# The causal layer's block solve: one PSUM bank for all heads, and hops as four full-array matmuls

## What is computed

```
logits = jnp.einsum('bhqd,bhkd->bhqk', q, k) * scale
probs = jax.nn.softmax(logits + causal_mask, axis=-1)
L = jnp.eye(s) - jnp.tril(probs, -1)
rhs = jnp.diagonal(probs, axis1=-2, axis2=-1)[..., None] * v
A = solve_triangular(L, rhs, lower=True)
out = A.transpose(0, 2, 1, 3).reshape(b, s, HID) @ Wd.T + bd
```

## Time and profile before

| what | value |
|---|---|
| median of 3 runs | 1507.68 us |
| the runs | 1501.56, 1507.68, 1512.19 us |
| span of the profiled execution | 1507.1 us |
| PE busy | 1237.4 us (82%) |
| DVE busy | 1035.0 us (69%) |
| ACT busy | 729.2 us (48%) |
| POOL busy | 628.0 us (42%) |
| mean granted clock of TensorE | 0.883 |

### The profile page before, as it was taken

The page is one execution under the profiler, slowest core; times in us unless marked ns, Lnnn a source line. Parts: engine busy times, 40 slices in busy tenths (PEclk is TensorE's granted clock), DMA queues, the critical chain, the costliest instruction groups (busy, mean ns, idle before and its releaser), DMA issues. The chain is left out here.

```text
span 1507.1 us, 30851 instructions
## 1 busy us (share of the span) xinstructions
PE 1237.4 (82%) x11642; PEld 673.8 (45%) x11642; DVE 1035.0 (69%) x2290; ACT 729.2 (48%) x1596; POOL 628.0 (42%) x838
## 2 busy tenths in 40 slices
PE   6656677779999988538889988988988799999976
PEld 2212232222333337424666766666666333333276
DVE  6699999979888955457446646645632588988653
ACT  3834334317766675313524523533442166676754
POOL 2279888853424215314423423223332524351244
PEclk9878888869999998758889879978997599999988
DMA  5378833023224022441421231141120231331213
GB/s 166 145 274 320 298 139 140 20 67 87 55 65 122 13 82 63 100 86 23 88 38 25 45 74 28 21 100 18 18 51 10 67 79 31 97 89 45 81 48 88
DMA packets 137737, 128.41 MB, mean 85 GB/s; under 512 B 92007, under 2 KB 123559, under 8 KB 132202
## 3 DMA queue, kind: packets, MB, share of 16 engines
q1 hardware_dynamic: 129536, 118.56, 28.6%
q0 software_dynamic: 2496, 5.13, 1.1%
q10 hardware_dynamic: 5558, 2.76, 0.9%
HBM read 105.61 MB, written 38.62 MB: 96 GB/s over the span
## 5 line engine op out<-in xcount | busy, mean ns | idle before, releaser
L1393 DVE TENSOR_REDUCE f_row_min<-f_ps 128x1 f32<-128x512 f32 x512 | 323.9, 676 | 55.6 <-PE f_ps L1720 55.2
L1283 ACT ACTIVATE f_e<-f_ps 128x512 f32<-128x512 f32 x512 | 282.8, 602 | 126.4 <-PE f_ps L1740 122.5
L1720 PE MATMUL f_ps<-f_operands 72*128 72x512 bf16 x512 | 205.4, 410 | 26.4 <-DMA f_operands<-k_scr 15.4
L1740 PE MATMUL f_ps<-f_operands 75*128 75x512 bf16 x512 | 189.5, 380 | 2.6 <-ACT f_e L1283 2.1
L790 PE MATMUL m_ps<-m_shared,sb_ident 128*128 128x512 f32 x256 | 136.8, 683 | 58.1 <-DVE m_shared L630 58.0
L363 POOL TENSOR_TENSOR m_drive<-m_du,m_ring 128x1024 f32<-128x1024 f32 x64 | 149.7, 2352 | 56.2 <-DVE m_ps L622 37.6
L495 ACT ACTIVATE m_ps<-m_delta,m_A 128x511 f32<-128x511 f32 x128 | 83.0, 681 | 131.7 <-DVE m_ps L622 109.0
L1751 PE MATMUL f_ps<-f_e,f_v_op 128*32 128x512 f32 x1024 | 136.4, 604 | 2.1 <-ACT f_e L1283 1.4
L2714 DVE TENSOR_TENSOR d_aT<-d_ps,d_aT 128x16 f32<-128x16 f32 x224 | 37.9, 169 | 140.9 <-PE d_ps L2892 140.7
L1720 PEld LDWEIGHTS f_ps<-f_operands 72*128 72x128 bf16 x512 | 51.3, 101 | 181.2 <-DVE f_row_min L1393 127.3
L2545 DVE TENSOR_REDUCE d_row_min<-d_ps 128x1 f32<-128x384 f32 (+3 forms) x176 | 106.3, 634 | 35.9 <-PE d_ps L2786 34.7
(11 more groups left out here) (298 smaller groups left out, 2345.3 us busy)
## 6 DMA issues: line engine op xcount, KB each, us to landing
m_ring<-bc_scr SPq DMA_DIRECT2D x32, 1024.0 KB, 5.4
f_rows_scr<-blank SPq DMA_DIRECT2D x2, 8707.5 KB, 30.8
f_wall<-f_wall SPq DMA_DIRECT2D x16, 578.0 KB
f_operands<-q_scr SPq DMA_DIRECT2D x32, 288.0 KB
f_operands<-k_scr SPq DMA_DIRECT2D x96, 96.0 KB
d_q_op<-q_scr SPq DMA_DIRECT2D x6, 576.0 KB
d_k_op<-k_scr SPq DMA_DIRECT2D x18, 192.0 KB
f_operands<-f_rows_scr SPq DMA_DIRECT2D x46, 64.5 KB, 1.8
```

What stands on the lines that cost most here:

```text
L1283: nc.scalar.activation(e_sb[:, n % 3, hh, :], ps[:, SCORE[(b * UNITS + u) % SCORE_BANKS], :], ACT.Exp, scale=SCALE).then_inc(s["e_out"], 1)
L1393: nc.vector.tensor_reduce(row_min[:, b % 2, u // TPB, u % TPB:u % TPB + 1], ps[:, MAXQ[(b * UNITS + u) % MAX_BANKS], :], AX.X, ALU.max, ne ...
L1720: nc.tensor.matmul(ps[:, MAXQ[n % MAX_BANKS], :], q_op(b, QK)[:, hd, t * P:(t + 1) * P], k_op(b, QK)[:, hd, :], start=True, stop=True).the ...
L1740: nc.tensor.matmul(ps[:, SCORE[n % SCORE_BANKS], :], k_op(b, QKS)[:, hd, t * P:(t + 1) * P], q_op(b, QKS)[:, hd, :], start=True, stop=True ...
```

## The change

All 16 heads now share one bank per tile (`STEP[n % 2]`). Head 4g + q has its 8 dimensions at row 32q + 8g of that bank, and the products of all groups g accumulate there. One step (a "hop") no longer multiplies by all rows so far: it takes the solution of the newest 16 or 32 tokens and adds what follows from it to all later columns. Odd hops take 16 tokens and touch 16 columns, even hops take a span of 32 tokens and touch the 96, 64 or 32 columns behind it. VectorE writes the left operand `a_hop` with four 32x32 transposes straight out of PSUM, one for each 32-row quadrant, so that it is block-diagonal over four heads x 32 tokens; a hop is then four matmuls of 128x128 float32 weights, one for each g. `mT` is stored to fit (`MT_COLS` = 320 columns instead of 512, 16 matmuls of 32 stationary columns per group of heads). ScalarE takes over the copy out of PSUM (`solved`, `from_earlier`), VectorE has three banks instead of two, and the scores, and the reciprocal of the sums (`inverted_at`, hook 8 for 7), sit at other hooks. The diff, cut to its core:

```diff
+PADDED = GROUPS * (GROUP * HEAD_COLS + HD)
+REST_AT = 256
+SPAN = 2 * BLK
+SPANS = P // SPAN
+MT_COLS = sum(P - SPAN * r for r in range(SPANS))
+HOPS = 2 * SPANS - 1
+HOP_AFTER = {3: 1, 5: 2, 7: 3, 9: 4, 10: 5, 11: 6, 12: 7}
-        STEP, TURN, TO_ACT, TO_DVE = (0, 1), (2, 3), (4, 5), (6, 7)
+        STEP, TURN, TO_ACT, TO_DVE = (0, 1), 2, (3, 4), (5, 6, 7)
-            return list(range(each * h, min(each * (h + 1), GROUPS_OF[t])))
+            return list(range(each * (h - 2), min(each * (h - 1), GROUPS_OF[t]))) if h >= 2 else []
-            return (-2, 4) if m == 0 else (m - 2, 7)
+            return (-2, 4) if m == 0 else (m - 2, 8)
...
 # ScalarE, multiplied
-                    nc.scalar.copy(mT[:, n % 2, i * GROUP:(i + 1) * GROUP, :].rearrange("p h i -> p (h i)"),
-                                   act_bank("mt", n, i)).then_inc(s["act_out"], 1)
+                    nc.scalar.copy(mT[:, n % 2, i, :], act_bank("mt", n, i)[:, 0:MT_COLS]).then_inc(s["act_out"], 1)
 # ScalarE: per half and step a copy of turned columns before; now
+                def solved(n):
+                    act.wait_ge(s["at_ps"], (HOPS + 1) * (n + 1))
+                    nc.scalar.copy(aT[:, n % 2, :], step_bank(n)).then_inc(s["at_sb"], 1)
+                def turned(n):
+                    act.wait_ge(s["an_ps"], turned_tiles(n))
+                    nc.scalar.copy(own_cols(a_all[:, n % TPB, :]), turned_cols()).then_inc(s["an_sb"], 1)
+                def from_earlier(n):
+                    act.wait_ge(s["g_ps"], later_tiles(n))
+                    nc.scalar.copy(gT[:, :], step_bank(n)).then_inc(s["gT_sb"], 1)
 # VectorE
-                def added(n, half, k):
-                    own = slice(k * BLK, (k + 1) * BLK)
-                    dve.wait_ge(s["at_ps"], 2 * (n * BLKS + k) + half + 1)
-                    nc.vector.tensor_tensor(aT[:, n % 2, half, own], ps[:, STEP[half], own], aT[:, n % 2, half, own],
-                                            ALU.add).then_inc(s["at_sb"], 1)
+                def turned_hop(n, k):
+                    dve.wait_ge(s["at_ps"], (HOPS + 1) * n + k)
+                    first = (k - 1) // 2 * SPAN
+                    for q in range(GROUP):
+                        own = slice(q * SPAN, (q + 1) * SPAN)
+                        bank = ps[own, STEP[n % 2], :]
+                        tokens = bank[:, first:first + SPAN]
+                        if k % 2:
+                            tokens = bank.rearrange("p (a c) -> p a c", a=2)[:, :, first:first + BLK]
+                        last = nc.vector.transpose(a_hop[own, :].rearrange("p (g c) -> p g c", g=GROUPS)[:, :, q * SPAN:q * SPAN + HD],
+                                                   tokens)
+                    last.then_inc(s["hop_in"], 1)
+                    for h in range(HOOKS):
+                        beside(n, h)
+                        if n >= 0 and n % TPB and h == 1:
+                            right_side(n)
+                        if n >= 0 and h == 2:
+                            turned_hop(n, 1)
+                        if n >= 0 and 1 <= HOP_AFTER.get(h, 0) < HOPS:
+                            turned_hop(n, HOP_AFTER[h] + 1)
 # TensorE, multiplied
-                    for hh in range(GROUP):
-                        hd = i * GROUP + hh
-                        last = nc.tensor.matmul(bank[:, hh * P:(hh + 1) * P], e_nat[:, n % 3, hd, :], xT[:, n % 2, hd, :],
-                                                start=True, stop=True)
+                    for r in range(SPANS):
+                        first = r * SPAN
+                        for q in range(GROUP):
+                            hd = i * GROUP + q
+                            last = nc.tensor.matmul(bank[q * SPAN:(q + 1) * SPAN, SPAN_AT[r]:SPAN_AT[r] + P - first],
+                                                    e_nat[:, n % 3, hd, first:first + SPAN], xT[:, n % 2, hd, first:P],
+                                                    start=True, stop=True)
+                def hop(n, k):
+                    if k == 1:
+                        pe.wait_ge(s["act_out"], all_mt(n))
+                    pe.wait_ge(s["hop_in"], HOPS * n + k)
+                    r = (k - 1) // 2
+                    cols = slice(BLK, SPAN) if k % 2 else slice(SPAN, P - r * SPAN)
+                    for g in range(GROUPS):
+                        last = nc.tensor.matmul(ps[:, STEP[n % 2], r * SPAN + cols.start:r * SPAN + cols.stop],
+                                                a_hop[:, g * P:(g + 1) * P],
+                                                mT[:, n % 2, g, SPAN_AT[r] + cols.start:SPAN_AT[r] + cols.stop],
+                                                start=False, stop=(g == GROUPS - 1), skip_group_check=True)
+                    last.then_inc(s["at_ps"], 1)
+                    if later:
+                        turned(n - 1)
+                    for h in range(HOOKS):
+                        beside(n, h)
+                        if later and h == 0:
+                            from_earlier(n)
+                        if later and h == 1:
+                            turn_right_side(n)
+                        if n >= 0 and h == 2:
+                            inverse(n)
+                        if n >= 0 and h in HOP_AFTER:
+                            hop(n, HOP_AFTER[h])
```

More of the change, by code:

```diff
@@ L1901 @@
 TURNS = BLKS - 1
-PADDED = NH * HEAD_COLS + 2 * HD
+PADDED = GROUPS * (GROUP * HEAD_COLS + HD)
+REST_AT = 256
+SPAN = 2 * BLK
+SPANS = P // SPAN
+SPAN_AT = [sum(P - SPAN * i for i in range(r)) for r in range(SPANS)]
+MT_COLS = sum(P - SPAN * r for r in range(SPANS))
+HOPS = 2 * SPANS - 1
+HOP_AFTER = {3: 1, 5: 2, 7: 3, 9: 4, 10: 5, 11: 6, 12: 7}
 HOOKS = 2 * TURNS
@@ L2885, in beside @@
                         project(goes_on(n, 5), h)
-                def side_by_side(half, lhs, rhs, rows, cols, done):
-                    for gl in range(2):
-                        for hh in range(GROUP):
-                            hd = head(half, gl, hh)
-                            last = nc.tensor.matmul(ps[hh * HEAD_COLS:(hh + 1) * HEAD_COLS, STEP[half], cols],
-                                                    of_head(lhs[rows, :], hd), rhs(hd), start=(gl == 0), stop=(gl == 1))
-                    last.then_inc(done, 1)
@@ L2896, in turn_half @@
-                def turn_half(half, src, done):
-                    nc.tensor.transpose(turn_bank(half), src[:, half, :], core.ident[:, :]).then_inc(done, 1)
-                def output(n):
-                    bank = dve_free("output", n)
-                    for half in range(2):
-                        last = nc.tensor.matmul(bank[:, 0:P], aT[:, n % 2, half, :], w["d_wd"][:, half, :],
-                                                start=(half == 0), stop=(half == 1))
-                    last.then_inc(s["dve_ps"], 1)
@@ L2906, in earlier_tiles @@
-                def earlier_tiles(n, half, out, tiles):
-                    t = n % TPB
-                    for gl in range(2):
-                        for j in tiles:
-                            for hh in range(GROUP):
-                                hd = head(half, gl, hh)
-                                last = nc.tensor.matmul(out[hh * HEAD_COLS:(hh + 1) * HEAD_COLS, :],
+                def output(n):
+                    pe.wait_ge(s["at_sb"], n + 1)
+                    nc.tensor.matmul(dve_free("output", n)[:, 0:P], aT[:, n % 2, :], w["d_wd"], start=True, stop=True).then_inc(
+                        s["dve_ps"], 1)
@@ L2913, in earlier_tiles @@
+                def earlier_tiles(n, tiles):
+                    t = n % TPB
+                    for j in tiles:
+                        for g in range(GROUPS):
+                            for q in range(GROUP):
+                                hd = g * GROUP + q
+                                last = nc.tensor.matmul(ps[q * SPAN:(q + 1) * SPAN, STEP[n % 2], 0:P],
                                                         of_head(a_all[:, j, :], hd), e_off[t][:, hd, j, :],
-                                                        start=(gl == 0 and j == tiles[0]), stop=(gl == 1 and j == tiles[-1]))
+                                                        start=(g == 0 and j == 0), stop=(g == GROUPS - 1 and j == t - 1))
@@ L2928, in inverse @@
-                def inverse(n, half):
-                    pe.wait_ge(s["gn_sb"], 2 * n + half + 1)
-                    side_by_side(half, g_nat[:, :], lambda hd: xT[:, n % 2, hd, :], slice(0, P), slice(0, P), s["at_ps"])
-                def product(n, half, k):
-                    pe.wait_ge(s["an_sb"], 2 * (n * BLKS + k - 1) + half + 1)
-                    own = slice(k * BLK, (k + 1) * BLK)
-                    rows = slice(0, k * BLK)
-                    side_by_side(half, a_nat[:, :], lambda hd: mT[rows, n % 2, hd, own], rows, own, s["at_ps"])
@@ new lines, in turn_right_side, with inverse @@
+                def turn_right_side(n):
```

(12 more changed lines are left out.)

205 lines of the change are left out of this document (69 added, 136 removed).

## The result

The changed kernel takes 1560.69 us (median of 4 runs, 1558.4 to 1563.95), the kernel before 1507.76 us beside it: a ratio of 1.0357 (95% interval 1.0326 to 1.0388), **53 us slower** where 26 us of gain were forecast. The time lies above the predicted range.

A forecast was written before the change was run, and what follows sets the result against it. TensorE's ordered list of work was taken as the bound. Gains of 8.1 us (pairs), 18.2 (seven covered tiles) and 2.5 (tiles 13, 14), less 2.7 (tile 15), gave 26 us: 1507 to 1481 us, range 1455 to 1508.

The forecast's parts named there:

- rival B: Rival, chance 0.2: waits for VectorE go almost wholly, hops cost 0.74 us, batch start does not hold; about 1457 us.
- D: Rival, chance 0.1: VectorE's transposes at 0.35 us overfill VectorE in tile 2 and lengthen round trips; slower, 1536 us.
- The transpose: On VectorE: one 32x32 transpose takes 0.14 us from start to start, the four of a hop 0.63 us.
- rival C: Rival, chance 0.18: the hop chain shows, transposes at 0.2 us cost 1 us per tile, 16 us in all; 1498 us.
- Hops: On TensorE: 0.89 us with 16 or 32 columns, 0.95 with 64, 1.05 with 96; 6.4 us added per tile.
- `mT`: On TensorE per tile: four groups in 32-column pieces at 0.75 us, 3.0 us in all, replace 4.4 us.
- The trade itself: On TensorE per tile: hops save nearly nothing, 6.3 us of products and turns removed against 6.4 us added.
- Batch start: Tiles 0/1, 4/5, 8/9: 30 us of queue and transfers stay; 2.5 of a pair's 5.2 us are given back.
- The third bank: VectorE's extra bank: with it, about 0.5 of the 1.46 us in which TensorE idles in tile 3 goes.
- Tile 15: Nothing lies between its hops: seven round trips of 1.93 us cost 3.3 us more, 0.6 comes back; +2.7 us.

The follow-up runs named there:

- e14: Changed kernel with odd hops streaming all later columns and two unneeded bf16 matmuls before each hop's wait, four transposes kept; not the layer's numbers: 1520.51 us, ratio 1.0113.
- e4: Changed kernel with odd hops streaming all later columns (16 to 112 instead of 16), same matmuls and loads; not the layer's numbers: 1537.00 us, ratio 1.0222.
- e5: Changed kernel with four unneeded bf16 matmuls of 256 columns before each hop's wait in tiles 13 to 15 only: 1550.73 us, ratio 1.0287.
- e9: Changed kernel with two unneeded bf16 matmuls of 256 columns before each hop's wait in all tiles, 224 in all: 1545.29 us, ratio 1.0247.
- e2: Changed kernel with each hop as 16 matmuls on 32x32 parts of the array instead of four full-array ones, four transposes kept: 1497.70 us, ratio 0.9936 to the kernel before.
- e1: Changed kernel with one transpose over 128 rows per hop instead of four, three diagonal blocks left out; not the layer's numbers: 1521.72 us, ratio 1.0122.
- e6: Changed kernel with each of the four transposes per hop done twice, the extra one into a spare buffer: 1594.22 us, ratio 1.0567.
- e7: Changed kernel with two of each hop's four full-array matmuls left out; not the layer's numbers: 1507.65 us, ratio 1.0009 to the kernel before.
- e3: Changed kernel with one transpose per hop into a dense left operand and hops of 16 matmuls on 32x32 parts: 1480.41 us, ratio 0.9826 to the kernel before.
- e10: Kernel before with only the new `mT` (32 stationary columns, copy of 320 columns); not the layer's numbers: 1501.36 us, ratio 0.9952.
- e12: e3 with the SP queue issuing the `e_nat` stores before the parts' stores and q and k loads, at batches 1 to 3: 1484.66 us, ratio 0.9856.
- e11: e3 with two VectorE banks instead of three: 1479.05 us, ratio 0.9812 to the kernel before.
- e13: Changed kernel with one transpose per hop and odd hops streaming all later columns; not the layer's numbers: 1497.97 us, ratio 0.9947 to the kernel before.

## Why the prediction was wrong, step by step

- **The step that failed is the clock.** All costs were summed at full clock, and the clock was spoken of only as something that "gives nothing back for shorter lists" (rival B). That it could be taken away was in no rival; the slower one, D, stood on the transposes alone. 147 us more at half clock are the failure: if TensorE paced the list all that time, half of it, 74 us, is lost (an estimate, and an upper end, since waits for transfers don't stretch); e14 gives 24 to 38 us from below. The gap between forecast and result in the layer is 52 + 26 = 78 us.
- **What brings it down**, as far as it is shown: the full-array hops with few columns together with the waits around them. With equal numbers of matmuls and loads, the clock is higher with more streamed columns (e4, 0.74 to 0.80) and with filler (e5, e9, e14); with tiled hops too (e2, 0.81). With shorter waits it is at half for 211 us, with longer ones for 321 (e1, e6). Half of the hops' matmuls taken away leaves it at 0.74 (e7), so their loads alone are not it. The share of time in which the profile shows TensorE busy doesn't tell it: 442.32 of 514.90 us, 0.86, in after; 0.89 before; 0.85 in e4 at a better clock; 0.75 in e3 at 0.86. The Trainium skill, page "TensorE: Matmul & The Clock Gate", section "What's actually happening", says that the clock follows how busy TensorE has been. Read with the busy time of the profile, that rule would set e3 below after, and the trace does not agree.
- **The transpose** is the second size: 0.14 us forecast from start to start, 0.22 measured. This is about rival C's price of 0.2, and its sign came, but not its time (1498): TensorE's waits for `a_hop` are 23.0 us, above the 20 named. The lines are from the table of waits of after:
```profile
DVE d_a_hop L2704 <- PE d_ps L2931: 105.0, 51, 3.2
...
PE d_ps L2931 <- DVE d_a_hop L2704: 23.0, 25, 2.0
```
The bounds of 0.169 and 0.725 us held it; the value taken lay below the lower one. Rows cost nothing: 32 x 32 takes 212 ns, 128 x 32 takes 211 (e3). The Trainium skill, page "VectorE: DVE Perf Modes", section "The three transpose paths", says that the transpose works on a grid of independent 32 x 32 blocks; e1 and e3 agree, one instruction transposes four quadrants in the time of one. Had the change been read so, its four instructions would have stood out as three too many.
- **Hops** at full clock: forecast 0.89, measured 0.85 here and 0.88 as the median of those with 16 columns; with 96 columns forecast 1.05, measured 0.92. **`mT`**: forecast 0.75 per group, measured 0.69. Both right. The saving in `mT` was right in size and wrong in worth: 7.6 us of 22 (e10, in the kernel before). At half clock a group takes 1.23 us, and in after at least 39 of the 64 groups lie there.
- **The trade itself** was seen, 6.3 against 6.4 us, and so was its alternative: the advice on fourfold tiling was quoted, and not priced as a kernel. The hop tiled in both directions takes 0.37 us for 16 columns, less than the 0.49 that was worked out for sixteen heads. The weighing was used against one term and not asked what it would do to the whole.
- **Batch start**: a longer wait of VectorE for the sums was forecast; in after it waits 6.0 us where it waited 21.3, as the slower list hides the transfers. In e3 it waits 54.1, and tiles 0 and 1 take 64.0 us, which fits the forecast of 65; that this chain is what bounds them is argued, since e12 moved the wait and gained nothing. Tiles 0 and 1 of after: measured 73.5, at clocks of 0.70 and 0.69 for 0.84 and 0.81. **The third bank**: 0.5 us per tile forecast, nothing measured (in e3, by e11).
- **Tile 15**: forecast 16.3 us (13.6 + 2.7), measured 22.9. A round trip is 2.9 us, 1.89 of hop with its tail and 0.98 of wait, where 1.93 were forecast, 1.14 of it hop and tail (0.89 + 0.25). So the hop at half clock is 0.75 of the 0.93 us of difference, and the rest goes with the longer transposes (0.88 us for 0.63).

Three errors against a sum of small savings: at full clock, with the transposes at rival C's price (17 us) and `mT` at its worth (some 14 us less), the forecast would have been about no change, by this estimate, and the clock then makes it a loss. **Open** is how the 13 us that e14 leaves split between the transposes and the added work, and why the transposes' removal gives 41 us in e1 where 17 were priced, a part of it being clock. Open is also what in a hop the clock answers to, since e4 and e14 change columns and the density of work together. Whether the numbers computed bear on the clock no run shows; e5 and e9 raise it with the layer's own numbers.

## What to carry to other kernels

When a change replaces many small matmuls by few with large loads and few moving columns, price TensorE at both clocks, as here 0.85 and 1.73 us for one hop, and make the clock's fall a rival of its own. Ask first whether the stationary operand's zeros are loaded for nothing: the block-diagonal form cost 0.85 us where the same blocks as 32 x 32 tiles cost 0.37, with 16 moving columns; with 96 it was 0.92 against 0.80. For VectorE's transposes count instructions, not rows.

## What was not expected of the hardware

- Added work can shorten a kernel: 24 us of filler, 8.7 us less (e9); wider hops, 23.0 us less (e4). Together, 38.5 us less (e14).
- Four 32 x 32 float32 transposes from PSUM take 0.88 us and do not overlap; one over 128 rows takes 0.21 us.
- Sixteen float32 matmuls of 32 x 32 x 16 take 0.37 us; four of 128 x 128 x 16 take 0.85 us at 2.4 GHz and 1.73 us at 1.2 GHz, all from start to start.
- Two edits that both free TensorE were nearly additive (58.8 of 64.2 us in the profiled runs, 62.7 of 62.7 in the medians, e13).
